# A four by four blur whose sixteen taps are divided among four engines instead of two

## The reference

```python
def _L1_conv_ref(x, kernel):            # kernel: 4 x 4
    xp = jnp.pad(x, ((0, 0), (0, 0), (2, 1), (2, 1)))
    k = jnp.flip(kernel)[None, None, :, :]
    xr = xp.reshape(N * C, 1, H + 3, W + 3)
    out = jax.lax.conv_general_dilated(xr, k, window_strides=(1, 1), padding='VALID', ...)
    return out.reshape(N, C, Ho, Wo)
...
x = x + _L1_conv_ref(_gn(x), L1_conv_kernel)
```

## Time and profile before

| | us |
|---|---|
| median of 3 runs | 7908.27 |
| lowest and highest | 7907.89 and 7908.82 |
| profiled execution, own time | 7900.45 |
| its span in the trace | 7898.5 |
| the blur, from 1040 to 1199 | 159 |

### The profile page before, as it was taken

How to read it: one execution, slowest core, us unless ns; L and a number is a source line. 1 busy time by engine, 2 the same in 40 slices (tenths; PEclk the granted TensorE clock), 3 DMA queues, 4 the chain that set the end, 5 groups by cost and what they waited for, 6 DMA issues and landing times. The chain is left out here.

```text
span 7898.5 us, 145982 instructions
## 1 busy us (share of the span) xinstructions
PE 6817.7 (86%) x42656; PEld 4640.5 (59%) x42656; DVE 6360.5 (81%) x9577; ACT 5763.4 (73%) x9016; POOL 5363.4 (68%) x3394
## 2 busy tenths in 40 slices
PE   5676787989968999999999999999999999999998
PEld 4444545767745666666666666665666666666666
DVE  3324184444439999999999999999999999999997
ACT  3416102222218999999999999999999999999997
POOL 3306000000009999999999999999999999999997
PEclk7878799999989999999999999999999999999998
DMA  1001000000010000000000000000000000000000
GB/s 65 22 3 38 0 0 0 0 0 0 0 58 10 1 1 1 1 1 1 10 1 1 1 1 1 1 27 1 1 1 1 1 2 2 3 3 3 4 4 5
DMA packets 75922, 55.73 MB, mean 7 GB/s; under 512 B 50776, under 2 KB 73464, under 8 KB 75032
## 3 DMA queue, kind: packets, MB, share of 16 engines
q1 hardware_dynamic: 72512, 53.88, 2.4%
q10 hardware_dynamic: 3288, 0.33, 0.0%
HBM read 37.80 MB, written 16.37 MB: 7 GB/s over the span
## 5 line engine op out<-in xcount | busy, mean ns | idle before, releaser
L1438 POOL TENSOR_TENSOR a_s<-a_s,a_v 128x784 f32<-128x784 f32 x1568 | 2910.3, 1856 | 429.5 <-ACT a_s L1650 414.0
L1474 PE MATMUL a_right_sides<-a_s,diag_d 128*128 128x392 f32 x6272 | 2281.7, 507 | 1.0 <-POOL a_s L1438 1.0
L1474 PEld LDWEIGHTS a_right_sides<-a_s,diag_d 128*128 128x128 f32 x6272 | 1130.6, 190 | 1035.9 <-issue 212.4
L1570 DVE SCALAR_TENSOR_TENSOR a_kan<-a_s,spline_c,a_kan 128x784 f32<-128x784 f32 x1568 | 1622.7, 1035 | 81.7
L1497 PEld LDWEIGHTS a_weighed<-a_V,a_probT 112*128 112x128 f32 x10976 | 1375.6, 193 | 162.2
L1431 POOL TENSOR_TENSOR a_inner<-a_inner,a_x 128x784 f32<-128x784 f32 x784 | 1456.8, 1858 | 0.0
L1497 PE MATMUL a_weighed<-a_V,a_probT 112*128 112x65 f32 x10976 | 1366.3, 270 | 0.0
L1650 ACT ACTIVATE a_s<-a_v 128x784 f32<-128x784 f32 x1568 | 1335.2, 852 | 4.6
L1641 ACT ACTIVATE a_v<-a_a 128x784 f32<-128x784 f32 x1568 | 1335.8, 852 | 0.3
L1486 PE MATMUL a_turned<-ident,a_prob 128*112 128x128 f32 x5488 | 856.7, 278 | 312.0 <-ACT a_probT L1657 305.7
L1461 PE MATMUL a_scores<-a_K,a_q 32*64 32x392 f32 x6272 | 699.6, 515 | 245.3 <-DVE a_kan L1552 214.6
(11 more groups left out here) (181 smaller groups left out, 6866.5 us busy)
## 6 DMA issues: line engine op xcount, KB each, us to landing
rows<-bias_rows_dram SPq DMA_DIRECT2D x112, 91.0 KB
X<-in_x_dram SPq DMA_DIRECT2D x4, 1568.0 KB, 15.8
a_q<-q_dram SPq DMA_DIRECT2D x392, 16.0 KB, 2.0
mask<-in_window_mask_dram SPq DMA_DIRECT2D x56, 98.0 KB
v_dram<-V SPq DMA_DIRECT2D x14, 227.5 KB, 2.3
a_V<-v_dram SPq DMA_DIRECT2D x4, 796.2 KB, 9.3
q_dram<-Q SPq DMA_DIRECT2D x14, 224.0 KB, 1.9
k_dram<-K SPq DMA_DIRECT2D x14, 224.0 KB, 1.9
```

Source lines behind the costliest of these rows:

```text
L1438: eng.tensor_tensor(s, s, v, ALU.mult).then_inc(cubed, 1)
L1474: mm = eng.matmul(up[:, j, 0:SUB], steps[i][:, :], cubes[g][:, SUB * j:SUB * (j + 1)], start=(i == 0), stop=(i == 1))
L1570: eng.scalar_tensor_tensor(F, banked((s1, s2)[j][g][:, :]), c[:, 3 + j:4 + j], F, ALU.mult, ALU.add).then_inc(left_added, 1)
```

## The change

`TAPS_PE` falls from 7 to 5, and a new `TAPS_POOL` = 5 names the next five taps. VectorE keeps the last six.

For the five, ScalarE writes the shifted window of `pad` times the tap's number into one of two new buffers `scaled` (Copy with a scale per partition). It waits for the buffer to be free (`scaled_used`). GpSimd adds the first two of them into `side`, then each further one to `side` in place, four tensor_tensor of 3136 columns per unit, each after the one before it has ended. `side` has two buffers; from unit 2 on GpSimd waits until the unit that used its buffer has been fully added. VectorE, after its six taps, waits for `side_summed`, adds `side` to X with one tensor_tensor over 3136 columns, and then adds the seven banks as before. ScalarE's queue is: padding of a unit, its five scaled images, padding of the next.

```diff
-    TAPS_PE = 7
+    TAPS_PE = 5
+    TAPS_POOL = 5
...
+        scaled = [st.enter_context(nc.sbuf_tensor(f"scaled{r}", [P, IMG, IMG], F32)) for r in range(2)]
+        side = [st.enter_context(nc.sbuf_tensor(f"side_sum{r}", [P, IMG, IMG], F32)) for r in range(2)]
...
             def _(pool):
                 for r in range(2):
                     pool.memset(pad[r][:, :, :], 0.0).then_inc(cleared, 1)
+                made = 0
+                for u in range(UNITS):
+                    acc = side[u % 2][:, :, :]
+                    if u >= 2:
+                        pool.wait_ge(added, CHUNKS * (u - 1))
+                    pool.wait_ge(scaled_made, made + 2)
+                    pool.tensor_tensor(acc, scaled[made % 2][:, :, :], scaled[(made + 1) % 2][:, :, :], ALU.add).then_inc(scaled_used, 2)
+                    made += 2
+                    for j in range(TAPS_POOL - 2):
+                        pool.wait_ge(scaled_used, made)
+                        pool.wait_ge(scaled_made, made + 1)
+                        pool.tensor_tensor(acc, acc, scaled[made % 2][:, :, :], ALU.add).then_inc(scaled_used, 1)
+                        made += 1
+                    pool.wait_ge(scaled_used, made)
+                    pool.sem_inc(side_summed, 1)
...
                     if u >= 2:
                         act.wait_ge(added, CHUNKS * (u - 1))
+                        act.wait_ge(scaled_made, TAPS_POOL * (u - 1))
                     act.activation(pad[u % 2][:, PAD:PAD + IMG, PAD:PAD + IMG], ...).then_inc(padded, 1)
+                    act.wait_ge(padded, u + 1)
+                    for j, (a, b) in enumerate(places[TAPS_PE:TAPS_PE + TAPS_POOL]):
+                        k = TAPS_POOL * u + j
+                        if k >= 2:
+                            act.wait_ge(scaled_used, k - 1)
+                        t = tap(a, b)
+                        act.activation(scaled[k % 2][:, :, :], pad[u % 2][:, a:a + IMG, b:b + IMG], ACT.Copy, scale=m.fir[:, t:t + 1]).then_inc(scaled_made, 1)
...
-                    for a, b in places[TAPS_PE:]:
+                    for a, b in places[TAPS_PE + TAPS_POOL:]:
...
                     dve.wait_ge(tapped, done)
+                    dve.wait_ge(side_summed, u + 1)
+                    dve.tensor_tensor(img, img, side[u % 2][:, :, :], ALU.add).then_inc(tapped, 1)
+                    done += 1
+                    dve.wait_ge(tapped, done)
                     for k in range(CHUNKS):
```

More of the change, by code:

```diff
@@ L818, in blur1 @@
         diag = [st.enter_context(nc.sbuf_tensor(f"diag_tap{j}", [P, P], F32)) for j in range(TAPS_PE)]
+        scaled = [st.enter_context(nc.sbuf_tensor(f"scaled{r}", [P, IMG, IMG], F32)) for r in range(2)]
+        side = [st.enter_context(nc.sbuf_tensor(f"side_sum{r}", [P, IMG, IMG], F32)) for r in range(2)]
         sums = [st.enter_context(nc.psum_tensor(f"tap_sums{k}", [P, 512], F32)) for k in range(CHUNKS)]
-        cleared, padded, tapped, diag_ready, pe_summed, added = (
-            sem(n) for n in ("pad_cleared", "padded", "tapped", "diag_ready", "pe_summed", "unit_added"))
+        cleared, padded, tapped, diag_ready, pe_summed, added, scaled_made, scaled_used, side_summed = (
+            sem(n) for n in ("pad_cleared", "padded", "tapped", "diag_ready", "pe_summed", "unit_added", "scaled_made", "scaled_used", "side_summed"))
         with nc.Block() as block:
@@ L833, in _ @@
                         act.wait_ge(added, CHUNKS * (u - 1))
+                        act.wait_ge(scaled_made, TAPS_POOL * (u - 1))
                     act.activation(pad[u % 2][:, PAD:PAD + IMG, PAD:PAD + IMG], m.X[:, u, :].rearrange("p (r c) -> p r c", c=IMG),
                                    ACT.Identity, bias=m.nbias[:, u:u + 1], scale=m.rstd[:, u:u + 1]).then_inc(padded, 1)
+                    act.wait_ge(padded, u + 1)
[5 more added lines that the diff above has]
+                        act.activation(scaled[k % 2][:, :, :], pad[u % 2][:, a:a + IMG, b:b + IMG], ACT.Copy, scale=m.fir[:, t:t + 1]).then_inc(scaled_made, 1)
+                act.wait_ge(scaled_made, TAPS_POOL * UNITS)
             @block.tensor
```

## The result

The changed kernel takes 7979.85 us (median of 4 runs, 7965.03 to 7981.8) against 7908.08 us before (4 runs, 7900.47 to 7908.82). The ratio is 1.0089, with a 95% interval of 1.0071 to 1.0106: slower by 0.9%, as forecast (7978).

A forecast was written before the change was run, and what follows sets the result against it. TensorE bound the blur at 36.8 us per unit; with exclusion, 1047.3 + 98.2 + 109.4 + 11.4 + 2.4 = 1268.7, 69.8 us later than 1198.94, added to the median 7908.27: 7978 us, range 7899 to 7992.

The forecast's parts named there:

- The exclusion: Blur: VectorE taps and side adds never run beside GpSimd adds, so held times sum; end 69.8 us later, chance 0.68.
- the blocked instructions of the earlier trace: First diag took 5.970 us instead of 0.269; near 76 us a memset and an xn: whole instructions wait for each other.
- just hidden: TensorE's last blur unit: 26.3 us plus 3 for a slow start, to end at 1265, when the side add ends.
- The rival of a slow TensorE: Blur: TensorE at the 1.2 GHz level all through a burst, 52.3 us per unit; kernel 7998 us, chance 0.05.
- GpSimd's add: Blur: one GpSimd add over 3136 columns, priced at 6.84 us, with 6.6 to 7.42 as limits.
- The sum: Blur with exclusion: VectorE and GpSimd held times plus bare adds and owner changes end at 1268.7, 69.8 us later.
- VectorE's own two-input work: Blur: 24 taps at 3.515 us and 4 side adds at 3.45, 98.2 us in all.
- sixteen GpSimd adds: Blur: 16 GpSimd adds at 6.84 us each, 109.4 us, all excluding VectorE's two-input work.
- PSUM adds bare of cover: Blur: seven PSUM adds of units 1 to 3 with no GpSimd add beside them, 3 x 3.8 = 11.4 us.
- changes of owner: Blur: some 24 switches between VectorE and GpSimd at 0.1 us each, 2.4 us.
- Free running with GpSimd's chain as bound: Blur without exclusion: GpSimd sets steps of 33.7 us, end at 1191.9, 7.0 us earlier; kernel 7901 us, chance 0.19.
- Partial sharing: Blur: taps and GpSimd adds both slow down but overlap, some half of the extra; kernel 7940 us, chance 0.08.

The follow-up runs named there:

- write-only: The change with each of the sixteen GpSimd adds replaced by a memset of 7500 columns, which reads nothing; blur 143.1 us.
- one-input kernel: The change with each GpSimd add replaced by a tensor_scalar reading only one scaled image; blur 155.4 us.
- PSUM kernel: The change with three scaled buffers and VectorE adding taps and side onto TensorE's sums in PSUM, in half units; blur 149.1 us, ratio 0.9983 against before.

## Why the prediction was right

**The exclusion** was the decisive step, and its conclusion holds. The write-only and the one-input kernel show the first half of it (a GpSimd instruction with one SBUF input is enough, one that only writes is not), the PSUM kernel the second half (a tap with one operand in PSUM collides with nothing).

The reason that I gave for it holds only in part. I had gone from the blocked instructions of the earlier trace rows to the taps by their read rate, since no row of before had a two-SBUF instruction beside a reading GpSimd instruction. But GpSimd's instructions in the earlier trace rows are memsets, which only write. By read rate alone, memsets should have shut out the taps as well, and the write-only kernel shows 3.485 us throughout. So the earlier trace rows show another pair than the one that decided here, and as evidence for this one they were no more than a hint (the xn near 76 us took 2.31 us, to 78.03; the longest, 2.354, is a later one). The Trainium skill, SBUF — State Buffer, "Who interferes with whom", states just this pair of conditions, and the traces agree as far as they go: 3.485 us per tap beside memsets, up to 9.94 beside adds. The conclusion came out right by that rule rather than by the earlier trace rows.

**TensorE and ScalarE.** 35 matmuls per unit took 28.0 to 29.6 us (26.3 and 3 for a start at the 1.2 GHz level were forecast), and the last unit's ended at 1261.4, with no wait of VectorE: just hidden, as said. The granted clock stood at 0.50 when TensorE restarted in units 1 to 3, after idle stretches of 29.4, 41.3 and 24.7 us, and rose 3.6 to 6.2 us later. The rival of a slow TensorE was held against by idle stretches in before "as long as the new ones"; those between 1198 and 1228 us were 18.1 and 10.8 us, so that argument was weak, though the rival did not occur. No table was loaded for Copy; a scaling took 2.93 us against 3.04.

**GpSimd's add** was priced at 6.84 us from two other shapes; undisturbed ones took 6.79 to 6.89.

**The sum** was too high by 8.8 us for the blur: 69.8 forecast, 60.8 measured (the first diagonal as origin: 228.0 forecast, 219.1 measured). Its terms:

| term | forecast | measured |
|---|---|---|
| first diagonal to first tap | 6.6 | 6.5 |
| VectorE's own two-input work | 98.2 | 97.3 + 0.9 between them |
| sixteen GpSimd adds | 109.4 | 102.9 (16 x 6.43) |
| PSUM adds bare of cover | 11.4 | 11.5 (15.2 less 3.7 covered) |
| changes of owner | 2.4 | none seen |

The mis-sized terms are the third and the last, and they are one thing. An add that is met costs VectorE 9.91 - 3.48 = 6.43 us, not its full 6.84: 0.4 us of it in all exclude nobody, and that leaves nothing for the changes of owner either. Taps and side adds took 163.5 + 33.1 = 196.6 us, 99.3 more than the 97.3 of the write-only kernel. That is fifteen adds at 6.43 and one at 2.75: the add that began at 1107.13 lay beside unit 0's PSUM adds first, and the tap behind them, in which it ended, took 6.23 us:

```profile
1111.07 6.23 DVE L889 SCALAR_TENSOR_TENSOR X<-pad,fir_taps,X 128x3136 f32<-128x3136 f32 x1
```

So one unit's PSUM adds were covered, as forecast, and nearly over their whole length: 6.43 less 2.75 is 3.7 us.

**The total** came out nearer than the sum deserves, and that is luck: 69.8 us forecast and 71.8 us between the medians, of which the blur gives 60.8. Between the lowest runs of both kernels the difference is 64.6. In the two profiled executions the rest lies mostly in the half-clock stretches of attention 3, which the prediction had not in view. The other executions have only a mean granted clock, which fits (0.954 in the change's run of 7965.03 us, 0.952 in those of 7980.84 and 7981.8). So that the rest between the medians, and the 7.8 us between the profiled execution and the median that I left unexplained in the prediction, come from them too is likely, not shown. That such stretches come without the change is shown; whether the change makes them more frequent isn't, and what sets them off stays open.

**The rivals.** Free running with GpSimd's chain as bound was put at 1191.9 - 1040.69 = 151.2 us for the blur; the write-only kernel, the nearest to it, took 143.1 with shorter GpSimd instructions (16 x 0.49 us more for 6.84 instead of 6.35 would make 150.9). Partial sharing is excluded by rows in which whole instructions wait. TensorE as the bound didn't occur. One figure there was off: to be faster by 0.2%, the free case needed an add under 6.3 us, not 6.4 (16 us less the 7.0, over 16 adds).

## What to carry to other kernels

Before work moves from VectorE to GpSimd, look at where the inputs of the VectorE instructions beside it lie. In these runs, with two SBUF inputs on VectorE and one or two on GpSimd, their times added up, and since an elementwise add took GpSimd twice as long as a whole multiply-and-add took VectorE (6.84 against 3.48 us), the move lost. With one VectorE operand in PSUM (a running sum on top of TensorE's) the same move gained.

## What the runs showed of the hardware

- A GpSimd add of 3136 columns keeps a two-input VectorE instruction out for 6.43 of its 6.84 us, a one-input GpSimd instruction for 2.43 to 2.47 of 2.81.
- Where each GpSimd instruction waits for the one before it, VectorE gets one instruction in between, and the two alternate at 9.97 us. The two memsets at 1040.65 of the earlier trace rows, with no wait between them, let nothing in; near 76 us VectorE's xn, begun beside a memset that ended at 76.38, got in ahead of the next one, which had begun at 76.32.
- A write-only GpSimd instruction shuts out the one-input tensor_scalar of the diagonals but not a two-input tap (3.485 us throughout).
- In attention 3 TensorE's clock falls to half for stretches of 6.8 us, zero to eight times per execution, at 2.6 to 3.4 us each. One and the same kernel had none in one execution and three, 7.8 us, in another; the most in any kernel here is eight, 23 us.
